# Attention's sums stored unturned, and normalised in the last phase

## The chip, the cores and the metric

One core of one Trainium2 chip. The metric is the device time of one execution in microseconds. Each figure is one number for the whole program: three phases that follow one another on five engines and overlap at their seams. The engines are TensorE (PE), VectorE (DVE), ScalarE (ACT), GpSimd (POOL) and SyncE (SP, which here issues all DMAs). Each runs its own list of instructions in order and waits on semaphores for the others.

## The reference

A block of three parts over x of shape (2, 2048, 256) in fp32:

```
x = x + 0.5 * ffn(layernorm(x))
x = x + attn(layernorm(x))
x = x + 0.5 * ffn(layernorm(x))
```

`ffn` is `square(relu(x W_fc^T)) W_proj^T` (1024 hidden channels), followed by five steps of a spiking neuron, whose count of spikes over 5 is the output. `attn` has 16 heads of 16 channels, rotary embedding on q and k, a causal softmax over 2048 keys, a bias on v and an output projection with bias:

```
scores = einsum('bhsd,bhtd->bhst', q, k) * scale      # causal mask
probs  = softmax(scores)
out    = einsum('bhst,bhtd->bhsd', probs, v)          # then x @ Wo.T + bo
```

## The kernel before, in words

**Phase A** (`feed_forward(True, ...)`) works in 8 chunks of CH = 512 tokens: the first ffn, the second layernorm, q, k and v. **Phase B** (`attention`) works in 8 groups: 2 batches times 4 groups of 4 heads. **Phase C** (`feed_forward(False, ...)`) does, for 8 chunks, the attention's output projection with its residual, then the second ffn.

*fp32 by halves.* A factor is split into a high part (`fp32r`, by ACT) and a low part (by DVE, value minus high); a product is three matmuls (hi x hi, lo x hi, hi x lo). `high` (L243 to 248) makes the high part, `low` (L359 to 362) the low part.

*Phase B.* A group has 4 steps j (512 queries each), a step has 4j + 4 blocks of 128 keys; a block is a slot, 40 slots a group, 320 in all (LAST). In each slot PE computes the block's scores for 4 heads (`scores`, L1078) into two buffers `s_ps`; ACT takes their exponentials into `probs` (L950); PE multiplies by the values (`products`, L1094) two slots later and sums in `o_ps`. The values carry a column of ones, so `o_ps` has, for each of 4 heads, 32 rows (VW): 16 channels, one row with the sum of the probabilities, 15 unused. Ahead of this, up to 20 slots earlier, PE computes all scores once more by 512 keys (`unit`, L1049) and DVE takes their maxima (L971, or L974 with the mask). These units go through three PSUM banks `m_ps` in a fixed order (`ring_order`, ORDER): the item number modulo 3 is the bank, PE waits for `max_read` of the item three before. From a step's maxima DVE makes shifts, which PE turns (`turn_shift`) and SP writes as rows of `qT`.

When a step's sums are complete, ACT copies `o_ps` to `osum` (`read_sum`, L938), with one buffer. Three slots into the next step an item "sums" stands in the ring: PE turns `osum` by four transposes of 128 x 128 (`turn_sums`, L1064), so that tokens are on the partitions, and DVE (`normalise`) takes the reciprocals of the sums (L1005, 16 numbers a partition) and multiplies (L1008) into `att`. SP stores this to `attn_tok` in DRAM (L816). The last two sums have their own bank (LATE); the very last is turned in phase C's first slot.

*Phase C.* A chunk is loaded from `attn_tok` (`load_attn`, L146) to `ain`, PE turns it back by eight transposes (`attn_turn`, `turn`, L572), ACT and DVE split it to `mT_hi` and `mT_lo`, PE projects (`attn_out`, L579), DVE adds the residual (`attn_sum`, L390), then stats, norm (`norm_scale` L340 to 348, `norm` L355), the transposes of `xn`, `xT_hi`/`xT_lo`, and the ffn. An iteration `it` has eight slots f (128 hidden channels each): PE does `up` f (six matmuls, L545) and `down` of three slots before (twelve, L563); ACT relu, square and `h_hi` (L294, L301, L303); DVE `h_lo` (L452); DVE also counts spikes of the chunk before (L373, one level a slot from f=3). `xT_hi` and `xT_lo` of the next chunk stand in f=7, and PE's `up` of f=0 waits for `xT_lo` (`pre_evac`). The attention's part runs ahead: in iteration `it`, f=1 has `attn_out(it+1)`, f=2 and f=4 the norm of chunk it+1, f=5 and f=6 the turn, `mT_hi` and `mT_lo` of chunk it+2.

The first two chunks' attention parts and the first norm are spread over the last group's 40 slots (`c_lead(x)`, x = slot - 280): each engine does its slot of phase B, then its piece of lead x. So x=19 is behind slot 299, the last that has maxima, and x=39 is behind the last slot.

Of the kernel before, what the change touches and what calls it, by code (L numbers as in the profile page):

```python
# [84 lines left out]
def feed_forward(first, src, dst, w, io, own, banks, s, meet):  # L85
# [15 lines left out]
    else:  # L101
        ain, xb, x2, bias = (own[n] for n in ("ain", "xb", "x2", "bias"))
# [22 lines left out]
    def sync(sp):  # L125
# [48 lines left out]
        def lead(x=None):  # L174
# [60 lines left out]
    def scalar(act):  # L235
# [5 lines left out]
        def high(which, c, hi, bank=tps):  # L241
# [24 lines left out]
        def lead(x=None):  # L266
# [8 lines left out]
            elif x == 21:  # L275
                high("a", 0, mT_hi, gps)
            elif x == 27:
                std(0)
            elif x == 29:
                high("a", 1, mT_hi, gps)  # L280
            elif x == 33:
                high("pre", 0, xT_hi, gps)

        def body(it, f):
# [21 lines left out]
            if not first and has(it, -2) and f == 5:  # L306
                high("a", it + 2, mT_hi, gps)
# [11 lines left out]
    def vector(dve):  # L319
# [39 lines left out]
        def low(which, c, hi, lo, bank=tps):  # L359
# [3 lines left out]
               .then_inc(s[which + "_evac"], 1)  # L363

# [48 lines left out]
        def lead(x=None):  # L413
# [12 lines left out]
            elif x == 22:  # L426
                low("a", 0, mT_hi, mT_lo, gps)
            elif x == 25:
# [3 lines left out]
            elif x == 28:  # L432
# [4 lines left out]
            elif x == 30:  # L437
                low("a", 1, mT_hi, mT_lo, gps)
            elif x == 34:
                low("pre", 0, xT_hi, xT_lo, gps)  # L440

        def body(it, f):
# [11 lines left out]
            if not first and f == 6 and has(it, -2):  # L454
                low("a", it + 2, mT_hi, mT_lo, gps)
# [27 lines left out]
            elif has(it, -1):  # L483
# [3 lines left out]
                if f == 4:  # L487
                    norm_scale(it + 1)
                    norm("pre", it + 1, it + 1, x2, xn, 0)

        return lead, body

    def gpsimd(pool):
# [22 lines left out]
        def lead(x):  # L516
# [3 lines left out]
            elif x == 27:  # L520
                add_bias(1)
# [14 lines left out]
    def tensor(pe):  # L536
# [12 lines left out]
        def down(it, f):  # L549

            if f == 0:
# [65 lines left out]
        def lead(x=None):  # L617
# [19 lines left out]
        def body(it, f):  # L637
# [26 lines left out]
            if not first and f == 5 and has(it, -2):  # L664
                attn_turn(it + 2)
# [15 lines left out]
MAX_FROM, MAX_TO, SUM = -20, 20, 3  # L681
# [60 lines left out]
LATE = [("sums", GROUPS - 1, j) for j in (NJ - 2, NJ - 1)]  # L742
assert [e for _, e in ORDER[-2:]] == LATE
# [5 lines left out]
def bank_of(e):  # L749
    return MB - 1 if e in LATE else ITEM[e] % MB  # L750
# [13 lines left out]
def attention(w, io, own, banks, s, ahead):  # L764
# [3 lines left out]
    probs, ident, bias, mask, masked, maxes, negmax, negparts, shiftT, osum, denom, att = (own[n] for n in (  # L768
        "probs", "ident", "bias_b", "mask", "masked", "maxes", "negmax", "negparts", "shiftT", "osum", "denom", "att"))
# [12 lines left out]
    def sync(sp):  # L782
# [177 lines left out]
    def vector(dve):  # L960
# [38 lines left out]
        def normalise(e):  # L999
            t, i = step_no(e[1], e[2]), ITEM[e]  # L1000
            dve.wait_ge(max_done, i + 1)
            if e in LATE:
# [375 lines left out]
```

## Time and profile before

| | |
|---|---|
| three runs, us | 1480.48, 1480.99, 1483.31 |
| the profiled execution, us | 1480.84 |
| its span, first to last instruction, us | 1479.1 |
| mean granted clock of TensorE | 0.949 |
| busy: PE, DVE, ACT, POOL | 91%, 77%, 58%, 15% |

Phase A ends at about 420 us, phase B at 1251.5 us, phase C at the span's end. Busy time is a share of the span; for PE it counts latencies too, so a PE that is busy all the time may still have small gaps. The granted clock is a share of 2.4 GHz: 0.50 is 1.2 GHz.

### The profile page before, as it was taken

The numbers are of one execution on the slowest core, as the hardware profiler recorded it, in microseconds if no ns is written. First come the engines' busy times: TensorE is split into PE (matmuls) and PEld (weight loads), VectorE is DVE, ScalarE is ACT, GpSimd is POOL, SyncE is SP. The second block draws the span as 40 slices with busy tenths as digits, with TensorE's granted clock in tenths as the row PEclk, the third lists the DMA queues.
The fourth block names the chain that finished last, engine by engine and source line by source line (L and its number), as shares of the span: only waits on it lengthen the run. The fifth ranks groups of instructions, "written<-read, shape, count | busy, mean of one in ns | idle before, by whom it ended". The sixth has DMA issues, their size and how long they took to land.

```text
span 1479.1 us, 22638 instructions
## 1 busy us (share of the span) xinstructions
PE 1345.1 (91%) x8416; PEld 809.8 (55%) x8416; DVE 1134.0 (77%) x2686; ACT 861.4 (58%) x1157; POOL 223.7 (15%) x205
## 2 busy tenths in 40 slices
PE   4988888967799999999999999999999998999996
PEld 3877777854444343444444444443443433999996
DVE  6566776796788888898898898888888851576675
ACT  4654455511166666676666666666666668665664
POOL 4002222241210110110110110110210110101100
PEclk9999999976699999999999999999999999999998
DMA  3123443772272160250340420610701011232312
GB/s 110 48 81 119 136 135 122 149 209 93 72 109 29 27 92 6 39 75 6 56 59 6 75 40 5 91 24 5 106 9 44 9 33 47 76 100 87 99 44 72
DMA packets 98598, 101.41 MB, mean 69 GB/s; under 512 B 39260, under 2 KB 78940, under 8 KB 96860
## 3 DMA queue, kind: packets, MB, share of 16 engines
q1 hardware_dynamic: 98488, 99.97, 29.7%
q8 instruction: 66, 1.08, 0.3%
q14 instruction: 44, 0.36, 0.1%
HBM read 60.16 MB, written 37.75 MB: 66 GB/s over the span
## 4 chain that ended last, share of the span: by engine, by line
PE 74%; DVE 19%; ACT 4%; issue 3%; DMA 0%; POOL 0%; SPq 0%; DVEq 0%; ACTq 0%
PE m_ps L1049 20%; PE o_ps L1094 18%; DVE maxes L971 9%; PE yps_c L563 6%; PE ups_c L545 6%; PE s_ps L1078 5%; PE ups_a L545 5%; PE yps_a L563 4%; PE gps_a L594 3%; DVE masked L974 3%; PE gps_a L579 2%; DVE turned_a L403 2%; PE gps_c L579 2%; ACT probs L950 1%; PE tps_a L572 1%
## 5 line engine op out<-in xcount | busy, mean ns | idle before, releaser
L950 ACT ACTIVATE probs<-s_ps 128x1024 f32<-128x1024 f32 (+3 forms) x640 | 542.0, 896 | 282.6 <-PE s_ps L1078 281.2
L971 DVE TENSOR_REDUCE maxes<-m_ps 128x1 f32<-128x512 f32 x768 | 490.2, 684 | 72.6 <-PE m_ps L1049 70.7
L1049 PE MATMUL m_ps<-kT,qT 64*128 64x512 f32 (+3 forms) x1280 | 455.6, 459 | 56.4 <-DVE maxes L971 37.9
L1049 PEld LDWEIGHTS m_ps<-kT,qT 64*128 64x128 f32 x1280 | 204.2, 192 | 412.1 <-DVE maxes L971 277.6
L1078 PE MATMUL s_ps<-qT,kT 64*128 64x512 f32 (+3 forms) x1280 | 317.0, 404 | 6.8 <-ACT probs L950 6.6
L1094 PE MATMUL o_ps<-probs,v_w 128*32 128x512 f32 (+3 forms) x2560 | 311.1, 559 | 0.1
L974 DVE CUSTOM_DVE_ANT_0 masked<-m_ps,mask 128x384 f32<-128x384 f32 (+3 forms) x512 | 233.6, 485 | 52.7 <-PE m_ps L1049 50.8
L919 POOL TENSOR_SCALAR_AFFINE_SELECT probs<-probs 128x512 f32<-128x512 f32 x128 | 81.3, 635 | 742.0 <-ACT probs L950 742.0
L1078 PEld LDWEIGHTS s_ps<-qT,kT 64*128 64x128 f32 x1280 | 170.0, 192 | 34.0 <-ACT probs L950 28.7
L452 DVE TENSOR_TENSOR h_lo_c<-hsq_c,h_hi_c 128x512 fp32r<-128x512 f32 x64 | 45.0, 703 | 71.1 <-ACT hsq_c L301 35.6
L294 ACT ACTIVATE relu_a<-ups_a 128x512 f32<-128x512 f32 x64 | 38.2, 596 | 99.5 <-PE ups_a L545 98.9
L452 DVE TENSOR_TENSOR h_lo_a<-hsq_a,h_hi_a 128x512 fp32r<-128x512 f32 x64 | 47.3, 739 | 58.5 <-ACT hsq_a L301 36.4
L1094 PEld LDWEIGHTS o_ps<-probs,v_w 128*32 128x32 f32 x2560 | 51.2, 109 | 73.6 <-issue 61.4
L294 ACT ACTIVATE relu_c<-ups_c 128x512 f32<-128x512 f32 x64 | 38.1, 596 | 73.5 <-PE ups_c L545 72.6
L501 POOL TENSOR_TENSOR rot_a<-turned_a 128x512 f32<-128x512 f32 x32 | 42.9, 1362 | 219.9 <-DVE turned_a L403 219.9
L563 PE MATMUL yps_a<-down_hi,h_hi_a 128*128 128x256 f32 x256 | 73.0, 285 | 2.2 <-ACT y_a L288 2.2
L563 PE MATMUL yps_c<-down_hi,h_hi_c 128*128 128x256 f32 x256 | 73.0, 285 | 0.0
L563 PE MATMUL yps_a<-down_lo,h_hi_a 128*128 128x256 f32 x256 | 72.5, 283 | 0.0
L563 PE MATMUL yps_a<-down_hi,h_lo_a 128*128 128x256 f32 x256 | 72.5, 283 | 0.0
L563 PE MATMUL yps_c<-down_hi,h_lo_c 128*128 128x256 f32 x256 | 72.4, 283 | 0.0
L563 PE MATMUL yps_c<-down_lo,h_hi_c 128*128 128x256 f32 x256 | 72.3, 283 | 0.0
L545 PE MATMUL ups_a<-xT_hi_a,up_hi 128*128 128x512 f32 x128 | 54.3, 424 | 2.5 <-DVE xT_lo_a L362 2.5
(128 smaller groups left out, 1923.3 us busy)
## 6 DMA issues: line engine op xcount, KB each, us to landing
qT<-qkT_parts SPq DMA_DIRECT2D x96, 128.0 KB
kT<-qkT_parts SPq DMA_DIRECT2D x48, 256.0 KB
qkT_parts<-qk_hi_a SPq DMA_DIRECT2D x32, 256.0 KB, 4.9
qkT_parts<-qk_lo_a SPq DMA_DIRECT2D x32, 256.0 KB, 4.6
table_a<-in_rot SPq DMA_DIRECT2D x8, 768.0 KB, 7.4
xin_a<-in_x SPq DMA_DIRECT2D x8, 512.0 KB, 3.9
xres_a<-in_x SPq DMA_DIRECT2D x8, 512.0 KB, 4.8
x<-xsum_a SPq DMA_DIRECT2D x8, 512.0 KB, 3.2
```

Source lines behind the costliest of these rows:

```text
L294: act.activation(relu[:, f % 2, :], ups[:, f % 2, :], ACT.Relu).then_inc(s["relu_done"], 1)
L452: dve.tensor_tensor(h_lo[:, f % HB, :], hsq[:, f % 2, :], h_hi[:, f % HB, :].bitcast(F32), ALU.subtract).then_inc(s["lo_done"], 1)
L545: last = pe.matmul(ups[:, f % 2, :], wt[:, c, f * P:(f + 1) * P], x[:, c, :], start=(i == 0), stop=(i == 3 * EC - 1))
L563: last = pe.matmul(yps[:, t, :], h[:, f % HB, t * P:(t + 1) * P], wt[:, f, :], start=(f == 0 and i == 0 and t % 2 == 0), stop=(f == FC - 1 ...
L579: last = pe.matmul(out, x[:, c, t * P:(t + 1) * P], wt[:, c, c0:c1], start=(i == 0), stop=(i == 3 * EC - 1))
L919: pool.affine_select(out=tile, in_=tile, compare_op=ALU.is_ge, fill=0.0, base=0, pattern=[[0, G], [1, P]], channel_multiplier=-1).then_inc ...
L950: act.activation(probs[:, b % PBUF, 2 * hp:2 * hp + 2, off:CH], s_ps[hp][:, :, off:CH], ACT.Exp, scale=D ** -0.5).then_inc(exp_done, 1)
L971: dve.tensor_reduce(out, m_ps[:, i % MB, 0:width], AX.X, ALU.max).then_inc(max_read, 1)
L974: dve.tensor_tensor_reduce(masked[:, i % MB, 0:width], m_ps[:, i % MB, 0:width], mask[:, CH - width:CH], 1.0, NEG, ALU.add, ALU.max, out). ...
L1049: pe.matmul(m_ps[:, i % MB, 0:width], qT[n % 2][r0:r0 + HR, j, hp, t * P:(t + 1) * P], kT[n % 2][r0:r0 + HR, hp, k * CH:k * CH + width], s ...
L1078: mm = pe.matmul(s_ps[hp][:, par, off:CH], kT[n % 2][r0:r0 + HR, hp, b * P:(b + 1) * P], qT[n % 2][r0:r0 + HR, j, hp, off:CH], start=True, ...
L1094: mm = pe.matmul(o_ps[VW * h:VW * (h + 1), off:CH], v_w[n % 2][:, b, h, :], probs[:, b % PBUF, h, off:CH], start=(b == 0), stop=(b == T * ...
```

## The change

- Phase B: the items "sums" leave the ring, and with them `turn_sums`, `normalise`, `att`, `denom`, LATE and the last sums in phase C's first slot. `osum` has two buffers, `read_sum` waits for the store of two steps before, and SP stores `osum` as it is, 128 rows (channels and the row of sums), to `sumsT` in DRAM.
- Phase C: `load_attn` makes four transfers a chunk: for each half k of the channels, the 8 heads' 16 rows to `sums`, and the row of the sums of each head, repeated for its 16 channels, to `denom`. DVE inverts `denom` and multiplies (`attn_norm`), ACT and DVE split `sums` (`attn_high`, `attn_low`). The transposes of `ain` go.
- The pieces of the lead move: `load_attn(0)` from x=0 to x=2; `attn_norm(0)` at x=19; `attn_high(0)` 20, `attn_low(0)` 21, `attn_out(0)` 22 (was 23), `attn_sum(0)` 24 (25), `attn_norm(1)` 25, `norm` 27 (28), `attn_high(1)` 28 (29), `attn_low(1)` 29 (30), the turn of `xn` 29 (31), `xT_hi` 30 (33), `xT_lo` 31 (34).
- `count` and `denom` change places in memory.

```diff
@@ feed_forward, sync
         def load_attn(c):
-            wait(sp, "a_T", c)
+            wait(sp, "a_evac", c)
             j, n = c % (NC // B), (c // (NC // B) + 1) * NG
-            sp.wait_ge(meet["att_out"][j % 2], 16 * (NC // B // 2 * (n - 1) + j // 2 + 1))
-            sp.dma_start(ain[:, :, :], rows(io["attn"], c)).then_inc(s["a_in"], 16)
+            sp.wait_ge(meet["osum_out"][j % 2], 16 * (NC // B // 2 * (n - 1) + j // 2 + 1))
+            if c == 0:
+                sp.wait_ge(meet["pv_done"], meet["blocks_but_last"])
+            heads = io["sumsT"][:, :, c * CH:(c + 1) * CH].rearrange("(k g) (h r) t -> k (g h) r t", k=EC, h=G)
+            for k in range(EC):
+                sp.dma_start(sums[:, k, :], heads[k, :, 0:D, :]).then_inc(s["a_in"], 16)
+                sp.dma_start(denom[:, k, :], heads[k, :, D:D + 1, :].broadcast_to([H // EC, D, CH])).then_inc(s["a_in"], 16)
@@ scalar
+        def attn_high(c):
+            wait(act, "a_norm", c + 1)
+            wait(act, "o_done", c)
+            act.activation(mT_hi[:, :, :], sums[:, :, :], ACT.Copy).then_inc(s["a_hi"], 1)
...
             if not first and has(it, -2) and f == 5:
-                high("a", it + 2, mT_hi, gps)
+                attn_high(it + 2)
@@ vector
+        def attn_norm(c):
+            wait(dve, "a_in", 16 * 2 * EC * (c + 1))
+            dve.reciprocal(denom[:, :, :], denom[:, :, :]).then_inc(s["a_rec"], 1)
+            wait(dve, "a_rec", c + 1)
+            dve.tensor_tensor(sums[:, :, :], sums[:, :, :], denom[:, :, :], ALU.mult).then_inc(s["a_norm"], 1)
+
+        def attn_low(c):
+            wait(dve, "a_hi", c + 1)
+            dve.tensor_tensor(mT_lo[:, :, :], sums[:, :, :], mT_hi[:, :, :].bitcast(F32), ALU.subtract).then_inc(s["a_evac"], 1)
...
                 if f == 4:
                     norm_scale(it + 1)
                     norm("pre", it + 1, it + 1, x2, xn, 0)
+                    if has(it, -2):
+                        attn_norm(it + 2)
@@ tensor
-        def attn_turn(c):
-            wait(pe, "a_in", 16 * (c + 1))
-            wait(pe, "x2_done", c)
-            turn(ain, "a_T", gps)
-
         def attn_out(c):
             wait(pe, "a_evac", c + 1)
+            wait(pe, "x2_done", c)
@@ attention
         def store(n, j):
             tok, group = place(n)
-            sp.wait_ge(max_read, ITEM["sums", n, j] + 1)
-            sp.dma_start(io["attn"][tok + j * CH:tok + (j + 1) * CH, group * G * D:(group + 1) * G * D]
-                         .rearrange("(t p) n -> p t n", p=P), att[:, j % 2, :, :]).then_inc(att_out[j % 2], 16)
+            sp.wait_ge(o_read, step_no(n, j) + 1)
+            sp.dma_start(io["sumsT"][group, :, tok + j * CH:tok + (j + 1) * CH], osum[:, j % 2, :]).then_inc(osum_out[j % 2], 16)
@@ attention, scalar
+            t = step_no(n, j)
             act.wait_ge(pv_done, block_no(n, j, T * j + T))
-            if (n, j) != (0, 0):
-                act.wait_ge(max_done, ITEM["sums", (NJ * n + j - 1) // NJ, (j - 1) % NJ] + 1)
-            act.activation(osum[:, :], o_ps[:, :], ACT.Copy).then_inc(o_read, 1)
+            wait(act, osum_out[j % 2], 16 * (t // 2))
+            act.activation(osum[:, j % 2, :], o_ps[:, :], ACT.Copy).then_inc(o_read, 1)
```

## Rows read from the trace of the kernel before

**Rows 1.** The page's chain of waits, shares of the span by engine and line.

```profile
PE 74%; DVE 19%; ACT 4%; issue 3%; DMA 0%; POOL 0%; SPq 0%; DVEq 0%; ACTq 0%
PE m_ps L1049 20%; PE o_ps L1094 18%; DVE maxes L971 9%; PE yps_c L563 6%; PE ups_c L545 6%; PE s_ps L1078 5%; PE ups_a L545 5%; PE yps_a L563 4%; PE gps_a L594 3%; DVE masked L974 3%; PE gps_a L579 2%; DVE turned_a L403 2%; PE gps_c L579 2%; ACT probs L950 1%; PE tps_a L572 1%
```

**Rows 2.** Windows: us, busy of PE, PEld, DVE, ACT, POOL, clock, DMA share, GB/s.

```profile
500.00:600.00 100.00, 95.55 (x631) 41.16 (x627) 87.53 (x235) 64.94 (x80) 14.83 (x18) 0.97 0.30 44
...
1200.00:1250.00 50.00, 44.19 (x289) 17.12 (x293) 10.70 (x27) 38.62 (x46) 8.92 (x9) 0.90 0.19 56
...
1350.00:1400.00 50.00, 49.99 (x337) 45.39 (x336) 35.04 (x63) 30.52 (x51) 5.67 (x2) 1.00 0.33 106
```

**Rows 3.** Groups by form: shapes, count, busy us, mean ns, idle before.

```profile
L1064 PE MATMUL m_ps<-ident,osum 128*128 128x128 f32 x128 | 20.9, 286 | 0.0
...
L1005 DVE RECIPROCAL denom<-m_ps 128x16 f32<-128x16 f32 x32 | 8.0, 251 | 7.1 <-PE m_ps L1064 6.9
```

**Rows 4.** Timeline of one step's sums: start, us, engine, line.

```profile
425.76 0.42 PEld L1064 LDWEIGHTS m_ps<-ident,osum 128*128 128x128 f32 x4 [0.25 <-issue]
425.77 0.66 PE L1064 MATMUL m_ps<-ident,osum 128*128 128x128 f32 x4
...
427.08 0.25 DVE L1005 RECIPROCAL denom<-m_ps 128x16 f32<-128x16 f32 x1
...
427.70 1.88 DVE L971 TENSOR_REDUCE maxes<-m_ps 128x1 f32<-128x512 f32 x3
```

**Rows 5.** Groups by form on DVE: small operations and one of 1024.

```profile
L381 DVE SCALAR_TENSOR_TENSOR xsum_c<-count_c,xres_c 128x1024 f32<-128x1024 bf16 x8 | 9.8, 1221 | 0.1
...
L340 DVE RECIPROCAL ln_c<-ln_c 128x4 f32<-128x4 f32 x8 | 1.4, 172 | 1.0 <-ACT ln_c L239 1.0
...
L340 DVE RECIPROCAL ln_a<-ln_a 128x8 f32<-128x8 f32 x5 | 1.0, 191 | 0.0
...
L342 DVE TENSOR_TENSOR ln_a<-ln_a 128x8 f32<-128x8 f32 x5 | 0.8, 168 | 0.2
```

**Rows 6.** Timeline of DVE in one iteration of phase C.

```profile
1348.36 0.69 DVE L452 TENSOR_TENSOR h_lo_c<-hsq_c,h_hi_c 128x512 fp32r<-128x512 f32 x1 [1.75 <-ACT hsq_c L301]
...
1352.40 0.69 DVE L452 TENSOR_TENSOR h_lo_c<-hsq_c,h_hi_c 128x512 fp32r<-128x512 f32 x1
...
1355.49 1.22 DVE L362 TENSOR_TENSOR mT_lo_c<-gps_c,mT_hi_c 128x1024 fp32r<-128x1024 f32 x1
...
1358.26 1.22 DVE L362 TENSOR_TENSOR xT_lo_c<-tps_c,xT_hi_c 128x1024 fp32r<-128x1024 f32 x1 [0.42 <-ACT xT_hi_c L248]
```

**Rows 7.** Timeline of PE: two starts of `up` f=0, and `ain`'s turn.

```profile
1331.87 0.50 PE L545 MATMUL ups_c<-xT_hi_c,up_hi 128*128 128x512 f32 x1
...
1350.55 1.03 PE L572 MATMUL gps_c<-ident,ain_c 128*128 128x128 f32 x8
...
1359.53 0.50 PE L545 MATMUL ups_c<-xT_hi_c,up_hi 128*128 128x512 f32 x1
```

**Rows 8.** Timeline of ACT in the same iteration.

```profile
1351.62 1.03 ACT L248 ACTIVATE mT_hi_c<-gps_c 128x1024 fp32r<-128x1024 f32 x1 [0.52 <-PE gps_c L572]
...
1361.23 0.60 ACT L294 ACTIVATE relu_c<-ups_c 128x512 f32<-128x512 f32 x1 [1.97 <-PE ups_c L545]
...
1362.40 0.62 ACT L303 ACTIVATE h_hi_c<-relu_c 128x512 fp32r<-128x512 f32 x1
```

**Rows 9.** Timelines of ACT, DVE and PE in slots 299 to 304.

```profile
1203.63 1.51 ACT L950 ACTIVATE probs<-s_ps 128x768 f32<-128x768 f32 x2 [0.69 <-PE s_ps L1078]
...
1200.71 0.67 DVE L409 TENSOR_TENSOR proj_lo_c<-stage_o_c,proj_hi_c 128x512 fp32r<-128x512 f32 x1
...
1211.19 0.73 PE L1078 MATMUL s_ps<-qT,kT 64*128 64x512 f32 x4
```

**Rows 10.** PE behind an idle stretch (timeline), and the clock there (windows).

```profile
1226.08 1.71 PE L1078 MATMUL s_ps<-qT,kT 64*128 64x512 f32 x4 [2.36 <-ACT probs L950]
...
1226.00:1232.00 6.00, 5.80 (x24) 1.47 (x24) 1.41 (x2) 5.32 (x7) 0.00 (x0) 0.50 0.56 179
```

**Rows 11.** DMA issues: size, median us to landing.

```profile
ain_c<-attn_tok SPq DMA_DIRECT2D x8, 512.0 KB, 3.9
```

More of the change, by code:

```diff
@@ L101, in feed_forward @@
     else:
-        ain, xb, x2, bias = (own[n] for n in ("ain", "xb", "x2", "bias"))
+        sums, denom, xb, x2, bias = (own[n] for n in ("sums", "denom", "xb", "x2", "bias"))
         split = [("o", own["stage_o"][:, :], proj_hi, proj_lo)]
@@ L425, in lead @@
                 split_low(0)
-            elif x == 22:
-                low("a", 0, mT_hi, mT_lo, gps)
-            elif x == 25:
+                attn_norm(0)
+            elif x == 21:
+                attn_low(0)
+            elif x == 24:
                 attn_sum(0)
@@ L431, in lead @@
                 norm_var(0)
-            elif x == 28:
+            elif x == 25:
+                attn_norm(1)
+            elif x == 27:
                 norm_scale(0)
@@ L436, in lead @@
                 norm("pre", 0, 0, x2, xn, 0)
-            elif x == 30:
-                low("a", 1, mT_hi, mT_lo, gps)
-            elif x == 34:
+            elif x == 29:
+                attn_low(1)
+            elif x == 31:
                 low("pre", 0, xT_hi, xT_lo, gps)
@@ L663, in body @@
                 up(it, 0)
-            if not first and f == 5 and has(it, -2):
-                attn_turn(it + 2)
         return lead, body
@@ L767, in attention @@
     qT, kT, v_in, v_w = ([own[f"{n}{p}"] for p in range(2)] for n in ("qT", "kT", "v_in", "v_w"))
-    probs, ident, bias, mask, masked, maxes, negmax, negparts, shiftT, osum, denom, att = (own[n] for n in (
-        "probs", "ident", "bias_b", "mask", "masked", "maxes", "negmax", "negparts", "shiftT", "osum", "denom", "att"))
+    probs, ident, bias, mask, masked, maxes, negmax, negparts, shiftT, osum = (own[n] for n in (
+        "probs", "ident", "bias_b", "mask", "masked", "maxes", "negmax", "negparts", "shiftT", "osum"))
     s_ps, m_ps, o_ps = banks
@@ L822, in moves @@
                     shift(n, j)
-                elif what == "sums":
+            for n, j in steps():
+                if g == min(block_no(n, j, T * j + T) + STORE, LAST):
                     store(n, j)
@@ L997, in shift_out @@
             dve.tensor_copy(shiftT[:, :], m_ps[0:2 * G * T, i % MB, 0:P]).then_inc(max_read, 1)
[L999 to L1002, printed above, removed]
-                dve.wait_ge(max_read, i)
-            sums = m_ps[:, bank_of(e), :].rearrange("p (g w) -> p g w", w=VW)
-            dve.reciprocal(denom[:, :].unsqueeze(2), sums[:, :, D:D + 1]).then_inc(denom_done, 1)
-            dve.wait_ge(denom_done, t + 1)
-            wait(dve, att_out[t % 2], 16 * (t // 2))
-            dve.tensor_tensor(att[:, e[2] % 2, :, :].rearrange("p t (h d) -> p (t h) d", d=D), sums[:, :, 0:D],
-                              denom[:, :].unsqueeze(2).broadcast_to([P, T * G, D]), ALU.mult)\
-               .then_inc(max_read, 1)
         pending = []
@@ L1032, in free_bank @@
         def free_bank(e):
[L1033 removed]
+            wait(pe, max_read, ITEM[e] - MB + 1)
         def unit(e):
@@ L1126, in end @@
                 products(*SLOTS[g])
-        def last_sums():
-            ring(ITEMS[LAST])
-        return slot, end, last_sums
+        return slot, end
     return sync, scalar, vector, gpsimd, tensor
@@ L1178, in build @@
     for n, shape in (("masked", [P, MB, CH]), ("maxes", [P, 2, 2, G // 2, T, NJ]), ("negmax", [P, G * T]), ("negparts", [P, 2, G * T]),
-                     ("shiftT", [2 * G * T, P]), ("denom", [P, T * G]), ("att", [P, 2, T, G * D])):
+                     ("shiftT", [2 * G * T, P])):
         b[n] = memory.take(n, shape)
@@ L1184, in build @@
     b["probs"] = memory.take("probs", [P, PBUF, G, CH])
-    b["osum"] = memory.take("osum", [P, CH])
+    b["osum"] = memory.take("osum", [P, 2, CH])
     assert memory.at <= rest
@@ L1192, in build @@
     for n, shape, dt in (("stage_o", [P, EC * E], F32), ("proj_hi", [P, EC, E], F32R), ("proj_lo", [P, EC, E], F32R), ("bias", [P, E], F32),
-                         ("ain", [P, T, E], F32), ("xin", [P, T, E], F32), ("mT_hi", [P, EC, CH], F32R), ("mT_lo", [P, EC, CH], F32R),
+                         ("sums", [P, EC, CH], F32), ("xin", [P, T, E], F32), ("mT_hi", [P, EC, CH], F32R), ("mT_lo", [P, EC, CH], F32R),
                          ("xb", [P, T, E], F32), ("x2", [P, T, E], F32), ("stats", [P, T, 6], F32), ("mv", [P, T, 2], F32),
@@ L1200, in build @@
                          ("hsq", [P, 2, CH], F32), ("h_hi", [P, HB, CH], F32R), ("h_lo", [P, HB, CH], F32R), ("y", [P, T * E], F32),
-                         ("count", [P, T * E], BF16)):
+                         ("denom", [P, EC, CH], F32)):
         c[n] = memory.take(n + "_c", shape, dt)
@@ L1204, in build @@
     memory = Memory(nc, probs)
-    for n in ("xres", "xsum"):
-        c[n] = memory.take(n + "_c", [P, T, E])
+    for n, shape, dt in (("xres", [P, T, E], F32), ("xsum", [P, T, E], F32), ("count", [P, T * E], BF16)):
+        c[n] = memory.take(n + "_c", shape, dt)
     with ExitStack() as ctx:
```

87 lines of the change are left out of this document (28 added, 59 removed).

## The prediction

> **What bounds the kernel now.** I read the chain of waits first, for the lines that set the end [rows 1]: TensorE (PE) has 74%, VectorE (DVE) 19%, ScalarE (ACT) 4%, DMA nothing. DVE's share is `maxes` (L971, L974), the attention's maxima. Then the busy times by stretch, since shares over the span mix stages [rows 2]. Between 500 and 600 us PE is busy 95.6 and DVE 87.5 of 100: they hand three PSUM banks to and fro, and both matter. In the last 20 slots (1200 to 1250) no maxima are left, DVE is busy 10.7 of 50 and ACT 38.6. In the last phase (1350 to 1400) PE is busy 49.99 of 50 and DVE 35.0. So three stages, and the change touches all.
>
> **1. Attention: the turned sums go.** 32 steps lose four transposes on PE (128 in all), and a reciprocal (0.25 us each) and a product on DVE [rows 3]. In one step [rows 4] the four transposes take 0.66 us with the last one's latency; at 0.14 us for one weight load to the next (their row in [rows 4] has 0.42 for the four, which overlap) it is 0.55 us of PE at the most. DVE starts the reciprocal at 427.08 and the next maximum at 427.70: 0.62 us, and never idles between. Both partners of the ring lose nearly the same, so whichever is late there gains about 0.6 us. 30 of the 32 steps lie among maxima (the last two come in slot 307 and behind the last slot, where DVE is idle): 30 x 0.6 = **-18 us**. Bounds: 12 us if part is lost to other waits of PE on bank 2 and 3, 22 us if PE's wait on `att` goes too. The store now goes out of `osum`, which has two buffers and is next written two steps, twelve slots at the least, later; it writes 128 rows of 2 KB where 512 pieces of 256 B were written, and ACT's copy no longer waits for PE. Nothing of that is waited for: 0.
>
> **2. The reciprocal of 128x1024.** It is new: DVE must now invert and multiply [128, 2, 512] for each of eight chunks. Three shapes of a reciprocal stand in the trace: 4 elements 172 ns, 8 elements 191 ns [rows 5], 16 elements 251 ns [rows 3]; a product of 8 costs 168 ns [rows 5]. So an element of a reciprocal costs far more than the 1.04 ns that 1221 ns for 1024 elements (about 157 ns fixed) make of an ordinary operation. Slopes: 4.75 ns from 4 to 8, 7.5 from 8 to 16, 6.6 over all. For 1024: 5.0 us by the first; 6.6 x 1020 + 172 = 6.9 us over all; 7.8 us by the second; and if the slope rises once more by as much, to 10.3 ns, 10.6 us. The 16-element row reads PSUM, so part of its excess may be the source; I take the middle, **R = 6.9 us**, bounds 5.0 and 10.6. The product is 1.2 us, as the two-input row of 1024 [rows 5].
> By the Trainium skill, "VectorE: DVE Perf Modes", section "First, the fixed hardware budget", a reciprocal is an iterative divide with a repeat count of 8. If that means 8 cycles of the page's 0.96 GHz for each element, the estimate is 8.5 us and the fixed part, and the sum below would end at 1545 us; the rows have shown 4.75 to 7.5 ns an element, not yet its 8.3.
>
> **3. The last phase, iterations 0 to 5.** PE loses eight transposes of `ain` (1.03 us with the last one's latency, 0.8 to the next start) [rows 7]. DVE gains R + 1.2 behind the normalisation of slot f=4. By sums this would fit: DVE's 35.0 of 50 [rows 2] is 19.4 of the 27.66 us between two starts of `up` f=0 (1331.87, 1359.53) [rows 7]; 19.4 + 8.1 = 27.5. But the order forbids it. ACT's `attn_high` of f=5 waits for the product (`a_norm`); queued behind it on ACT are relu, squares and `h_hi` of f=6, relu of f=7 and `xT_hi`; on DVE, behind the product, `h_lo` of f=5, `h_lo` of f=6 (which needs ACT's), `mT_lo`, a spike, `xT_lo`; PE's `up` f=0 waits for `xT_lo`. Before, this chain ended at 1358.26 + 1.22 = 1359.48 and PE started at 1359.53: it has no slack. After, from PE's start (1331.87): 16.49 to `h_lo` f=4 (1348.36), 4.04 until DVE has normalised (1352.40) [rows 6]; R + 1.2; `attn_high` 1.03 and relu to `h_hi` 1361.23 to 1363.02 = 1.79 [rows 8]; `h_lo` 0.65, `mT_lo` and a spike 2.35 (1355.49 to 1357.84, where the idle 0.42 before `xT_lo` begins), `xT_lo` 1.22 [rows 6], about 0.15 of semaphores. That is 28.9 + R = 35.8 us against 27.66: +8.1, six times **+48.6 us** (37 at R = 5.0, 71 at R = 10.6). With h_hi and h_lo in four buffers, PE can go on to `down` f=4 and then waits.
>
> **4. The clock.** In this chain PE waits about 5 us for `up` f=0: from the product's end it is 7.2 us (1.03 + 1.79 + 0.65 + 2.35 + 1.22 + 0.15), and PE has only `down` f=5 left, which follows `h_lo` f=5 (0.65) and takes about 1.5. In the last 20 slots PE idled 2.36 us and was then granted 0.50 (1.2 GHz) for the six us from 1226 to 1232 [rows 10]; six us at half rate lose 3.0 of PE's work. Here PE sets the time between `up` f=0 and f=4, so it would be paid: I take 2.5 us a time, six times **+15 us** (0 if the level holds, 20 at most).
>
> **5. The last slots (lead).** `attn_norm(0)` stands at x=19, behind `split_low` (1200.71 + 0.67 = 1201.4); with R + 1.2 it ends at 1209.5, `attn_high(0)` at x=20 at 1210.6. Queued behind it on ACT are the exponentials of slot 301, which before began at 1203.63: +7.0 [rows 9]. PE's two score buffers are then full, `attn_out(0)` at x=22 follows slot 302, and slot 304's scores, before at 1211.19, come at about 1217.8: +6.6. The second `ain` turn and the turn of slot 307 are gone, 0.8 and 0.55 us of PE: -1.4. The new hole of some 7 us before `attn_out` can cost the clock there, +1. `attn_norm(1)` (x=25) starts near 1220, 3.8 us after `attn_out(0)` has ended, and would end near 1229, before ACT's x=28 (near 1231): hidden, but by 2 us only; at R = 10.6 some of it shows. Sum **+6** (bounds 0 and +12). The removed last turn is 0.55 us of PE, within that.
> **Loads.** SP issues four transfers of 256 KB a chunk for one of 512 KB: +0.5 MB, at the start of an iteration; in front of `load_x`. SP passes them as soon as `mT_lo` of the chunk before is done (f=6), some 20 us before their use at f=4; a load of `ain` landed after 3.9 us in the median [rows 11]: 0. `load_attn(0)` moves from x=0 to x=2 and waits for the end of group 6, 17 slots ahead of use: 0. `load_attn(1)` is issued near 1211.5 and needed near 1220, the only close one.
>
> **Sum**, against the profiled execution (1480.84, span 1479.1 and 1.7 around it): 1480.84 - 18 + 48.6 + 15 + 6 = 1532.4; the median of the runs shown, 1480.99, lies 0.15 above that execution. **Forecast 1532 us.**
>
> **Rivals.**
> - *The slope goes on rising* as it did from 4.75 to 7.5 ns; halfway from 7.5 to 10.3, at 8.9 ns, R = 9.2. Against it: the 16-element row reads PSUM. 6 x (28.9 + 9.2 - 27.66) = 63, clock 15, lead 8, attention -18: 1549 us. The Trainium skill's repeat count (same page and section) would end between this and the forecast.
> - *Cheap reciprocal*: what looks like a slope is fixed cost, and 1024 elements take 1.2 us as other operations do. Then the chain is 28.9 + 1.2 = 30.1, +2.4 x 6 = 15, lead nothing, the clock held: 1480.8 - 18 + 15 = 1478 us, barely on the other side. It decides at R near 1.8, without clock loss: 6 x (R + 1.24) = 18. Against it: 19 ns for four elements more, and another 60 for eight more.
> - *DVE's idle time takes it all*: if ACT and DVE were far enough ahead, the iteration would be DVE's 27.5 us, as now, and the lead 0: 1480.8 - 18 - 1 = 1462 us, faster. For it: DVE idles 30% of the phase. Against it: `xT_lo` ends 0.05 us before PE's `up` now.
> - *The loads come late*: the broadcast rows of `denom` take over 20 us to land, and DVE waits 3 to 6 us more in each of six iterations: 1550 to 1568. For it: a shape that the trace doesn't show; against it: the 3.9 us of `ain` [rows 11].
>
> **Chances.** Forecast 0.55, rising slope 0.30, loads late 0.06, cheap reciprocal 0.05, all hidden 0.04. Range: R = 5.0 with half of the clock's loss gives 1480.8 - 20 + 37 + 7 + 3 = 1508, and with none of it 1500; R = 10.6 gives 1480.8 - 15 + 71 + 15 + 10 = 1562. So 1500 to 1560, of which about 2 in 10 are left out, most of it below. A measurement of this kernel tells about 0.2%, 3 us. Slower 0.90, the same 0.02 (between the cheap reciprocal with and without its clock loss), faster 0.08.
>
> **What would show it.** The row of the new reciprocal, 128x1024, eight times: 6.9 us each. In 1300 to 1350 PE's busy share falls from all to under 85%, and a stretch at 0.50 appears. Two starts of `up` f=0 are 35 to 38 us apart for six iterations, then 27.7. ACT waits for DVE `sums` at `attn_high`, PE's weight load waits for DVE `xT_lo` some 5 us at a time. The attention's stretch up to the last maximum is about 18 us shorter. A row below 2 us for the reciprocal makes the forecast wrong; a period of 27 us beside a long reciprocal makes part 3 wrong.

## The result: slower by 2.4%, 1518.9 us

The changed kernel took 1518.91 us (median of 4 runs, 1515.61 to 1519.26) against 1482.15 (1480.48 to 1483.62); ratio 1.0243, 95% interval [1.0224, 1.0263]. Forecast was 1532, range 1500 to 1560. The profiled execution has a span of 1516.9 us, 37.8 more than before.

Its page begins with the busy times. Then the chain of waits, whose rows answer to [rows 1]:

```profile
PE 1328.0 (88%) x8224; PEld 798.4 (53%) x8224; DVE 1174.4 (77%) x2638; ACT 860.2 (57%) x1157; POOL 223.2 (15%) x205
...
PE 66%; DVE 24%; ACT 6%; issue 4%; DMA 0%; DVEq 0%; POOL 0%; SPq 0%; ACTq 0%
PE m_ps L1040 19%; PE o_ps L1077 17%; DVE maxes L977 9%; PE ups_a L572 5%; PE ups_c L572 5%; PE s_ps L1061 5%; PE yps_a L589 4%; DVE masked L980 3%; PE yps_c L589 3%; PE gps_a L620 3%; DVE denom_c L378 3%; PE gps_a L605 2%; DVE turned_a L425 2%; PE gps_c L605 2%; PE tps_a L598 1%
```

PE has less to do (17 us less busy, 192 matmuls less) and the kernel is slower: PE's share of the chain fell from 74% to 66%, and a new member stands in it, `denom_c` L378, the reciprocal, with 3%. DVE's share of busy time, 77%, has not moved at all; it would have told nothing. The windows that answer to [rows 2]:

```profile
500.00:600.00 100.00, 95.13 (x641) 39.97 (x640) 88.48 (x239) 68.29 (x83) 14.82 (x18) 1.00 0.30 50
...
1200.00:1250.00 50.00, 45.63 (x295) 25.03 (x288) 17.52 (x38) 38.42 (x52) 5.38 (x5) 0.93 0.16 48
...
1300.00:1350.00 50.00, 41.91 (x243) 37.04 (x243) 31.85 (x43) 21.61 (x37) 5.67 (x2) 0.85 0.40 124
1350.00:1400.00 50.00, 42.06 (x257) 37.27 (x257) 36.52 (x61) 23.49 (x40) 2.84 (x1) 0.90 0.21 64
```

In the last phase PE is busy 42 of 50 us instead of 50, at a mean clock of 0.85 to 0.90 instead of 1.00: it waits, and the waits cost the clock. Who is waited for stands in the list of that phase's waits (the last three figures are us in total, times, and the longest in us):

```profile
ACT mT_hi_c L258 <- DVE sums_c L380: 54.9, 6, 9.2
...
PEld ups_c L572 <- DVE xT_lo_c L372: 25.9, 7, 4.9
...
PEld yps_c L589 <- DVE h_lo_c L477: 23.7, 6, 4.4
```

To part the 37.8 us by stage, two events mark the seams: the last maximum's `negmax` (DVE, step j = 3 of each group) and PE's first `up` of the last phase. From the timeline of DVE, before (the last two of eight), then after:

```profile
1093.31 0.22 DVE L981 TENSOR_REDUCE negmax<-maxes 128x16 f32<-128x64 f32 x1
1199.41 0.22 DVE L981 TENSOR_REDUCE negmax<-maxes 128x16 f32<-128x64 f32 x1
```

```profile
558.99 0.22 DVE L987 TENSOR_REDUCE negmax<-maxes 128x16 f32<-128x64 f32 x1
660.23 0.22 DVE L987 TENSOR_REDUCE negmax<-maxes 128x16 f32<-128x64 f32 x1
763.76 0.22 DVE L987 TENSOR_REDUCE negmax<-maxes 128x16 f32<-128x64 f32 x1
...
1173.29 0.22 DVE L987 TENSOR_REDUCE negmax<-maxes 128x16 f32<-128x64 f32 x1
```

and of PE, before and after:

```profile
1251.53 0.50 PE L545 MATMUL ups_c<-xT_hi_c,up_hi 128*128 128x512 f32 x1
```

```profile
1231.09 0.50 PE L572 MATMUL ups_c<-xT_hi_c,up_hi 128*128 128x512 f32 x1
```

| stage | before | after | difference | forecast |
|---|---|---|---|---|
| to the last maximum | 1199.4 | 1173.3 | -26.1 | -18 |
| from there to the first `up` (lead) | 52.1 | 57.8 | +5.7 | +6 |
| last phase | 227.6 | 285.8 | +58.2 | +63.6 |
| span | 1479.1 | 1516.9 | +37.8 | +51.6 |

**The reciprocal.** The group of the new instruction, by form (count, busy us and mean ns, idle time before it):

```profile
L378 DVE RECIPROCAL denom_c<-denom_c 128x1024 f32<-128x1024 f32 x8 | 52.3, 6543 | 0.0
```

It takes 6.54 us, eight times, and DVE is never idle ahead of it: the loads were in time.

**One iteration.** The same places on DVE and ACT as in [rows 6, 8], with the two starts of `up` f=0 at its ends, as in [rows 7]. DVE, where the first row is `h_lo` of f=4 and the last `xT_lo`:

```profile
1318.60 0.69 DVE L477 TENSOR_TENSOR h_lo_c<-hsq_c,h_hi_c 128x512 fp32r<-128x512 f32 x1 [1.75 <-ACT hsq_c L311]
...
1322.65 6.55 DVE L378 RECIPROCAL denom_c<-denom_c 128x1024 f32<-128x1024 f32 x1
1329.23 1.23 DVE L380 TENSOR_TENSOR sums_c<-sums_c,denom_c 128x1024 f32<-128x1024 f32 x1
1330.37 0.68 DVE L477 TENSOR_TENSOR h_lo_c<-hsq_c,h_hi_c 128x512 fp32r<-128x512 f32 x1
...
1336.18 1.22 DVE L372 TENSOR_TENSOR xT_lo_c<-tps_c,xT_hi_c 128x1024 fp32r<-128x1024 f32 x1
```

ACT, and then PE's weight loads:

```profile
1330.49 1.06 ACT L258 ACTIVATE mT_hi_c<-sums_c 128x1024 fp32r<-128x1024 f32 x1 [9.15 <-DVE sums_c L380]
```

```profile
1299.62 0.29 PEld L572 LDWEIGHTS ups_c<-xT_hi_c,up_hi 128*128 128x128 f32 x1 [4.85 <-DVE xT_lo_c L372]
1337.45 0.29 PEld L572 LDWEIGHTS ups_c<-xT_hi_c,up_hi 128*128 128x128 f32 x1 [4.71 <-DVE xT_lo_c L372]
```

ACT stands still for 9.15 us until the product is there, PE for 4.7 us until `xT_lo` is. The distance is 37.83 us, against 27.66 in [rows 7]. From PE's start to `h_lo` of f=4 it takes 18.98 us (1299.62 to 1318.60), where the prediction had 16.49: the 2.49 us more are what the low clock costs (e3_keep_busy, below). From there to the reciprocal it is 4.05 us, as worked out.

### The profile page after: what moved, and what is told of

It is laid out like the page before. It is cut to its first block, busy times and chain, and to the rows that moved or that the text cites. A ratio compares the mean times of both kernels' runs of the same rounds, so it can differ in the third digit from the quotient of the medians.

```text
span 1516.9 us, 22165 instructions
## 1 busy us (share of the span) xinstructions
PE 1328.0 (88%) x8224; PEld 798.4 (53%) x8224; DVE 1174.4 (77%) x2638; ACT 860.2 (57%) x1157; POOL 223.2 (15%) x205
## 4 chain that ended last, share of the span: by engine, by line
PE 66%; DVE 24%; ACT 6%; issue 4%; DMA 0%; DVEq 0%; POOL 0%; SPq 0%; ACTq 0%
PE m_ps L1040 19%; PE o_ps L1077 17%; DVE maxes L977 9%; PE ups_a L572 5%; PE ups_c L572 5%; PE s_ps L1061 5%; PE yps_a L589 4%; DVE masked L980 3%; PE yps_c L589 3%; PE gps_a L620 3%; DVE denom_c L378 3%; PE gps_a L605 2%; DVE turned_a L425 2%; PE gps_c L605 2%; PE tps_a L598 1%
## 5 line engine op out<-in xcount | busy, mean ns | idle before, releaser
L1040 PE MATMUL m_ps<-kT,qT 64*128 64x512 f32 (+3 forms) x1280 | 443.5, 454 | 57.6 <-DVE maxes L977 39.6
L1040 PEld LDWEIGHTS m_ps<-kT,qT 64*128 64x128 f32 x1280 | 198.8, 190 | 408.7 <-DVE maxes L977 279.2
L1061 PE MATMUL s_ps<-qT,kT 64*128 64x512 f32 (+3 forms) x1280 | 312.7, 399 | 12.8 <-ACT probs L956 12.5
L572 PE MATMUL ups_c<-xT_hi_c,up_hi 128*128 128x512 f32 x128 | 57.4, 449 | 24.0 <-DVE xT_lo_c L372 24.0
```

What stands on the lines that cost most here:

```text
L572: last = pe.matmul(ups[:, f % 2, :], wt[:, c, f * P:(f + 1) * P], x[:, c, :], start=(i == 0), stop=(i == 3 * EC - 1))
L1040: pe.matmul(m_ps[:, i % MB, 0:width], qT[n % 2][r0:r0 + HR, j, hp, t * P:(t + 1) * P], kT[n % 2][r0:r0 + HR, hp, k * CH:k * CH + width], s ...
L1061: mm = pe.matmul(s_ps[hp][:, par, off:CH], kT[n % 2][r0:r0 + HR, hp, b * P:(b + 1) * P], qT[n % 2][r0:r0 + HR, j, hp, off:CH], start=True, ...
```

## The experiments

In all, "distance" is the time between two PE starts of `up` f=0 of the last phase; `e1` to `e3` are edits of the changed kernel.

### The length of the reciprocal (e1_narrow)

```diff
-dve.reciprocal(denom[:, :, :], denom[:, :, :])
+dve.reciprocal(denom[:, :, 0:32], denom[:, :, 0:32])
```

> The changed kernel (1518.9 us, last phase 285.8 us from PE's first `up`) with the reciprocal cut to 64 of its 1024 elements; the other sums stay undivided, so part of the normalisation is left out. Everything else, the product at f=4 too, stays in its place. Theory (the long reciprocal stands in the chain up f=0, norm at f=4, product, mT_hi on ACT, relu and h_hi f=6, xT_lo, next up f=0, which is 28.9 + R us): R falls from 6.54 to 0.5 to 0.6, the chain to 29.5, so the distance of two up f=0 falls from 37.7 to 29.5 us if the clock holds, 31.7 if PE's remaining wait of some 3 us still costs it; the lead gives back about 6 us. Together 1518.9 - 6 x 6 to 8.2 - 6 = 1464 to 1477 us. Rival 1 (the reciprocal's length is hidden and four loads a chunk or the extra traffic cost the time): no change, 1515 to 1519. Rival 2 (DVE's idle time takes what is left, order does not matter): distance 27.7 or less, 1458 or less.

Measured 1474.65 us (ratio to before 0.9954, [0.9939, 0.9969]). The reciprocal's row, and two of the five equal distances:

```profile
L378 DVE RECIPROCAL denom_c<-denom_c 128x64 f32<-128x64 f32 x8 | 4.3, 543 | 2.2 <-DMA denom_c<-sumsT 2.2
```

```profile
1283.68 0.19 PEld L572 LDWEIGHTS ups_c<-xT_hi_c,up_hi 128*128 128x128 f32 x1 [2.77 <-DVE xT_lo_c L372]
1314.60 0.19 PEld L572 LDWEIGHTS ups_c<-xT_hi_c,up_hi 128*128 128x128 f32 x1 [2.77 <-DVE xT_lo_c L372]
```

The distance is 30.9 us, and the iteration behind the sixth takes 28.24 against 26.78 before: 1.45 us of clock. 30.93 - 1.45 = 29.48, the chain's 28.9 + 0.54 = 29.44. So 44 us of the kernel hang on six microseconds of an instruction. The loads and the traffic are those of the changed kernel, so rival 1 falls; the one wait for a load, the 2.2 us in the row above, lies ahead of the last phase (at 1193 us). And it is not all: with the short reciprocal the distance is still 3.3 us over the 27.66 of before, 1.45 of it clock and the rest the chain, since the product at f=4 still stands ahead of ACT's `mT_hi`. Rival 2 (DVE's idle time takes what is left) falls too.

### The place (e2_early)

```diff
@@ vector, body
             if not first and f == 6 and has(it, -2):
                 attn_low(it + 2)
+            if not first and f == 1 and has(it, -2):
+                attn_norm(it + 2)
...
-                    if has(it, -2):
-                        attn_norm(it + 2)
```

> The changed kernel with nothing left out, only the normalisation (reciprocal and product, 7.8 us) of iterations 0 to 5 moved on DVE from behind the norm of f=4 to behind h_lo of f=1. Theory (order): ACT's mT_hi at f=5 no longer waits for it; what is then late is DVE itself, whose work in an iteration is 19.4 + 7.8 = 27.2 us and is nearly all strung together from f=1 on, so a distance of 28 to 30.5 us instead of 37.7: 1518.9 - 6 x 7.2 to 9.7 = 1461 to 1476 us. Rival (it is the amount, DVE 7.8 us more in a phase it has no room for, wherever it stands): 34 us or more, above 1497.

Measured 1484.32 us (1.0007, [0.9991, 1.0023]): no change against before, 35 us under the changed kernel, but 8 above my expectation. The distances are 28.9, 31.65, 30.16, 31.28, 30.17, 31.31, at or a little over the upper end of the expected 30.5, and far from the rival's 34. The three over 31 each hold one stretch at 0.50 (near 1291, 1353 and 1414 us), the two of 30.2 hold none, so that 1.1 to 1.5 us of the three go with the clock. Two weight loads of `up` f=0:

```profile
1296.88 0.19 PEld L572 LDWEIGHTS ups_c<-xT_hi_c,up_hi 128*128 128x128 f32 x1 [0.20 <-DVE xT_lo_c L372]
1327.04 0.19 PEld L572 LDWEIGHTS ups_c<-xT_hi_c,up_hi 128*128 128x128 f32 x1 [0.59 <-DVE xT_lo_c L372]
```

and, among the waits from 1240 to 1450 us:

```profile
ACT ln_c L246 <- DVE ln_c L343: 30.8, 6, 6.2
...
PEld tps_c L598 <- DVE xn_c L365: 14.3, 6, 2.9
```

Now ACT waits for DVE's part of the norm, and PE for the normalised `xn`, not for the attention's halves: here the long instruction delays what stands behind it at f=1 too, and f=1 is only the better place. Seven of the ten us between a distance of 37.7 and before's 27.7 went by the place alone, with the same work. The kernel's other excess lies ahead of the last phase: its last maximum came at 1178.6 us instead of 1173.3, with the same code up to there (see part 1 below).

### The clock (e3_keep_busy)

```diff
+        def keep_busy(c):
+            wait(pe, "x2_done", c)
+            for i in range(17):
+                pe.matmul(gps[:, 0, :], up_hi[:, 0, 0:P], up_hi[:, 0, 0:CH], start=True, stop=True)
...
+            if not first and f == 7 and has(it, -2):
+                keep_busy(it + 2)
             if f == 0 and has(it, 0):
+                if not first and 1 <= it <= NC - 2:
+                    keep_busy(it + 1)
                 up(it, 0)
```

> The changed kernel, nothing left out, with 17 extra matmuls of 512 columns (3.9 us at the full clock) on PE in each of its two waits of an iteration: behind down f=4, where it waits 4.2 us for h_lo, and ahead of up f=0, where it waits 4.6 us for xT_lo. Their results are overwritten and never read. Theory (2.25 us of each distance are the low clock behind these waits): the granted clock stays at 1.00 through the last phase, the distances fall from 37.7 to 35.4 us, the iteration behind the sixth from 29.0 to 26.8: -13.5, 1505 us. Rival (the 2.25 us are something else, such as a longer way from xT_lo to PE or late relus): distances 37.7 or more, 1519 to 1525.

Measured 1506.1 us (1.0167, [1.0147, 1.0186]): 34 matmuls an iteration whose results nobody reads make the kernel 13 us faster. In the profiled execution the last phase alone is 13.1 us shorter (272.7 instead of 285.8); its whole span is only 8.4 us shorter, as what lies ahead of that phase took 4.7 us longer. In the changed kernel the window from 1332 to 1342, with the second wait and what follows it, had a clock of 0.52; with them the last phase is at 1.00:

```profile
1332.00:1342.00 10.00, 5.58 (x18) 4.32 (x17) 6.02 (x7) 5.16 (x10) 0.00 (x0) 0.52 0.38 114
```

```profile
1300.00:1440.00 140.00, 136.94 (x836) 120.49 (x835) 105.95 (x147) 65.21 (x112) 9.69 (x4) 1.00 0.30 91
```

```profile
1338.22 0.19 PEld L572 LDWEIGHTS ups_c<-xT_hi_c,up_hi 128*128 128x128 f32 x1 [1.19 <-DVE xT_lo_c L372]
1373.57 0.19 PEld L572 LDWEIGHTS ups_c<-xT_hi_c,up_hi 128*128 128x128 f32 x1 [1.19 <-DVE xT_lo_c L372]
```

The distance is 35.35; the chain of the prediction with the measured R is 28.9 + 6.54 = 35.44. The iteration behind the sixth takes 26.79, as before the change. So 2.25 to 2.5 us of each distance from the third to the sixth, and as much behind it, were the low level. Where they are paid shows in PE's rows, from the start of `up` f=0 to the first matmul behind its twelve, in the changed kernel and with the matmuls added:

```profile
1337.45 0.79 PE L572 MATMUL ups_c<-xT_hi_c,up_hi 128*128 128x512 f32 x1 [4.42 <-DVE xT_lo_c L372]
1342.69 0.29 PE L605 MATMUL gps_c<-proj_hi_c,mT_hi_c 128*128 128x256 f32 x1
```

```profile
1338.22 0.50 PE L572 MATMUL ups_c<-xT_hi_c,up_hi 128*128 128x512 f32 x1 [0.77 <-DVE xT_lo_c L372]
1341.08 0.28 PE L605 MATMUL gps_c<-proj_hi_c,mT_hi_c 128*128 128x256 f32 x1
```

The twelve take 5.24 us instead of 2.86: 2.38 us. The low level itself lasted some 10 us, but PE waited for nearly half of them, and that half cost nothing more. It fell near 1332.4, behind the first wait (for `h_lo`) and before the second (for `xT_lo`); this run fills both, so which of them brings the fall is not parted.

### Which partner of the ring gains (e6_turn_one, e7_no_product)

Both are edits of the kernel before.

```diff
@@ e6_turn_one, turn_sums
-            for t in range(T):
+            for t in range(1):
@@ e7_no_product, normalise
+            if t > 1:
+                dve.sem_inc(max_read, 1)
+                return
```

> The kernel before (distance of two groups' last maxima 106.05 us, each with one stretch at the low clock) with one of the four transposes of osum in each sum's item; the other three columns blocks are left out of the result. It takes 0.42 us of PE a step and nothing of DVE, and the item keeps its place and bank. Theory (at a sum's item both partners of the ring are late, and each one's saving shows only as far as the other's): 0.2 to 0.4 us a step, 0.8 to 1.7 a group, 104.4 to 105.3 us, -6 to -13 us in all. Rival 1 (DVE alone sets the attention's pace): distance 106.0, no change. Rival 2 (PE alone): 104.4 or less.

> The kernel before with DVE's product of 256 elements left out in all but the first two steps (att keeps old values); the four transposes, the reciprocal of 16 and the item stay. It takes 0.37 us of DVE a step and nothing of PE. Theory (as for the run with one transpose): 0.2 to 0.37 us a step, 0.8 to 1.5 a group, 104.5 to 105.3 us. Rival 1 (DVE alone): 104.5, the whole 0.37 a step. Rival 2 (PE alone): 106.0. Together with that run: if either saving alone gives nothing, only both together give the 2.54 us a group of the change.

With one transpose the kernel took 1481.69 us (0.9994, [0.9984, 1.0003]), without the product 1471.41 (0.9928, [0.9902, 0.9955]). The `negmax` rows of two neighbouring groups in each:

```profile
881.31 0.22 DVE L981 TENSOR_REDUCE negmax<-maxes 128x16 f32<-128x64 f32 x1
987.25 0.22 DVE L981 TENSOR_REDUCE negmax<-maxes 128x16 f32<-128x64 f32 x1
```

```profile
458.15 0.22 DVE L981 TENSOR_REDUCE negmax<-maxes 128x16 f32<-128x64 f32 x1
563.36 0.22 DVE L981 TENSOR_REDUCE negmax<-maxes 128x16 f32<-128x64 f32 x1
```

Three transposes of four gone from PE: 105.9 us a group instead of 106.05, 0.04 us a step of the 0.42 saved. The product gone from DVE: 105.2 in the groups with the same clock as before, 0.21 us a step of 0.37. So my theory that either saving shows in part was wrong for PE, whose transposes were nearly free while the item stood, and right for DVE at its lower end; that DVE alone sets the pace would have given 0.37. The whole item gone gives 0.63 a step (part 1 below), as much as DVE's 0.62 of [rows 4], but 0.04 and 0.21 do not add up to it: no run parts the rest, which holds the reciprocal of 16, the last transpose and the item's turn in the ring.

### A version that beats both (e5_compact), and two attempts on it

The sums of a chunk, 16 heads by 512 tokens, are 128 x 64 numbers when each is there once; the change inverts each of them 16 times. Here SP loads them as 128 x 64, DVE inverts that one iteration earlier, SP stores 16 rows, and `denom` is loaded repeated from those; the product stands at f=1.

```diff
+        def load_comp(c):
+            ...
+            heads = io["sumsT"][:, :, c * CH:(c + 1) * CH].rearrange("g (h r) (q t) -> (g h) r q t", h=G, q=8)
+            sp.dma_start(comp[:, c % 2, :], heads[:, D, :, :]).then_inc(s[f"c_in{c % 2}"], 16)
+        def attn_rec(c):
+            ...
+            dve.reciprocal(crec[:, c % 2, :], comp[:, c % 2, :]).then_inc(s["a_rec"], 1)
+        def store_rec(c):
+            ...
+            sp.dma_start(io["recT"][:, c * CH:(c + 1) * CH].rearrange("h (q t) -> h q t", q=8), crec[:, c % 2, :])\
+              .then_inc(s[f"r_out{c % 2}"], 16)
```

> A version meant to be better, nothing left out: the sums of the probabilities of a chunk are loaded as 128 x 64 (each once, not 16 times), inverted by one reciprocal of 64 elements an iteration earlier, stored to DRAM as 16 rows, and loaded repeated from there; the product of 1024 stands behind h_lo of f=1. Theory: the last phase is bound by PE again, without the turns of ain, 26.6 us an iteration against 27.66 before the change; attention keeps its 26 us; the lead loses nothing: 1482.2 - 26 - 6 = 1450 us. Rival 1 (attention's 26 us come in part from the clock and don't recur with other phases): up to 1457. Rival 2 (the round through DRAM, two DMAs and SP's waits, is late): DVE waits for the loads at f=1 and the distance is 29 us or more, above 1465.

Measured 1451.04 us (0.9787, [0.9771, 0.9803]). It is 31 us faster than before and 68 faster than the changed kernel.

```profile
L409 DVE RECIPROCAL crec_c<-comp_c 128x64 f32<-128x64 f32 x8 | 4.3, 542 | 0.0
```

```profile
1254.00:1416.00 162.00, 160.65 (x1056) 145.21 (x1055) 126.33 (x216) 99.18 (x167) 12.00 (x5) 1.00 0.37 105
```

PE is busy 160.65 of 162 us at the full clock, distances 26.8 to 27.4. The 0.2 to 0.8 us over 26.6 are not fully explained. DVE waits 8.0 us in all for the repeated rows ahead of the product, but only 3.1 of them in the last phase (1.42, 1.35 and 0.29 us, in the distances 27.4, 27.3 and 27.0); a distance of 27.1 has no such wait.

> The compact version (1451.0 us, distances 27.4, 27.3, 27.0, 27.1, 26.8 in the last phase) with the product of 1024 behind h_lo of f=3 instead of f=1. At f=1 DVE waited 8 us in all for the repeated rows to land, and the product took 1499 ns in the mean instead of 1225, beside GpSimd's add. Theory (both slow it and push xT_lo of f=7 past PE): at f=3 the loads have landed and GpSimd is done, the distances fall to 26.8, -1 to -2 us in all, 1449 to 1450. Rival (DVE's work between f=3 and f=7 is what is late, so that a product there is worse than at f=1): distances 28 or more, 1455 or more.

The edit is `f == 3` for `f == 1`. Measured 1454.18 us (0.9808, [0.9794, 0.9823]), no better: the product took 1214 ns instead of a mean of 1499 (one of 3.43 us, beside GpSimd's add, and seven of 1.2), DVE no longer waited for the rows in this phase, and the distances are 27.9, 27.4, 27.7, 26.8, 26.8, 26.8: three longer, three as good. The theory of a gain falls, and the rival's figure was not reached either.

> The compact version with the score matmuls of the first two slots of each group done three times over (the same values again, 16 matmuls more a group, about 1.5 us of PE): the place where PE waits for maxima of 128 columns and, 1 to 3 us later, the granted clock falls to 0.50 for 4 to 8 us in six of seven groups. Theory (these waits bring the fall, and a fall costs 2.3 us of a group): the stretches go, groups take 101.2 us and the added matmuls' share not hidden, 0.5 to 1 us: 6 x 2.3 - 8 x 0.75 = -8, 1443 us. Rival (the fall comes from the whole stretch of narrow matmuls before it, and these few change nothing): stretches stay, and the matmuls cost up to 12 us, 1455 to 1463.

```diff
-                mm = pe.matmul(s_ps[hp][:, par, off:CH], ...)
+                for _ in range(3 if j == 0 and b < 2 else 1):
+                    mm = pe.matmul(s_ps[hp][:, par, off:CH], ...)
```

Measured 1460.78 us (0.9853, [0.9838, 0.9869]): slower than e5_compact. The clock fell in every group all the same, and groups took 102.9 to 105.0 us. The expectation also counted wrong: in e5_compact only four of the seven distances (table below) hold such stretches, not six, and all seven are 11 us over seven undisturbed ones. The time is the rival's: the matmuls before decide, or the place is the wrong one; what brings the fall in the attention stays open.

## Why the prediction was right, and where its sizes were off

**The direction and the mechanism** (parts 2 and 3) held, with one thing left open (the first distance, below). R was read as 6.9 us from three short reciprocals; it is 6.54. The longer ones give the law: (6543 - 543) / 960 = 6.25 ns an element over 0.14 us, which makes 0.17 and 0.19 us for 4 and 8 as in [rows 5], and 0.24 for 16, where [rows 3] has 0.25. The overall slope of 6.6 was thus nearly right, and the rival "the slope goes on rising" falls: a few ns above and below the law at 4, 8 and 16 elements had looked like a rise. Whether the 8 ns at 16 come from its source in PSUM no run shows. What also falls is the reading of the Trainium skill's repeat count of 8 ("VectorE: DVE Perf Modes", "First, the fixed hardware budget") as 8 cycles an element, an estimate of 8.3 ns: the measured rows decide, 6.25 ns. The chain 28.9 + R was confirmed in three kernels, at two values of R: 35.35 (R = 6.54, e3), 29.48 (R = 0.54, e1, less the clock), and 37.7 less 2.25 in the changed kernel. That DVE's sum would fit in its idle time was rightly set aside.

**Part 4, the clock:** 2.5 us a time was forecast; 2.24 was paid by the iteration behind the sixth, where nothing else differs (29.02 against 26.78), and e3 took back 13 us of the 15. The six us at half rate of [rows 10] were near the right size for the work that PE does at the low level (5.24 us here), though the level itself lasts longer, over the wait too.

**Part 3, the number of times:** the last phase was forecast 5.4 us too slow. 0.36 us of R, six times, is 2.2. The clock is paid six times, but one distance late, from the second to the one behind the sixth, and came to 13.2 us (e3) instead of 15: 1.8. The rest, 1.2 us, is in the first distance, which grew by 6.6 us, where the chain with the measured R had 7.8; why is not shown.

**Part 5, the lead:** +6 forecast, +5.7 measured. `attn_norm(0)` held ACT for 6.20 us (its `mT_hi` began at 1183.02, 9.7 behind the last maximum) where 7.0 were worked out. The smaller terms of this part were not measured one by one.

**Part 1, the attention, is the mis-sized term:** -18 us (12 to 22) forecast, -26.1 measured. The saving itself was right: a group took 106.05 us, each with one stretch of some 7 us at the low clock (seven of seven), and takes 103.50 where such a stretch is left: 2.55 us, 0.63 a step, 17.8 in seven groups. But in three of the seven groups the stretch is gone, and these take 101.24: 2.27 us less each, 6.8 together (the rest, 1.5 us, lies in the first group and in the shorter stretch of the second). I had taken the clock of the attention as given. The kernel before has one stretch in each of the seven, and so has e6_turn_one, whose item still stands. Six kernels with the changed attention have between one and three groups with none, and most of them one with two, not in the same groups from kernel to kernel. So fewer stretches seem to come with the change, for a reason that no run shows. The part of luck in this one execution shows in the sums: the seven distances make 717.0 us in the changed kernel and to 719.4 to 721.4 in the five others, against 742.3 before. Of the 26.1 us some 2 to 4 are thus luck.

| kernel | distances of neighbouring groups, us |
|---|---|
| before | 106.1 106.0 106.0 106.0 106.1 106.1 106.1 |
| after | 102.7 101.2 103.5 101.3 103.5 101.2 103.5 |
| e1_narrow | 102.6 101.2 103.5 102.6 101.2 103.5 106.0 |
| e2_early | 102.7 101.2 103.5 102.6 105.1 102.6 102.7 |
| e3_keep_busy | 102.7 106.0 101.2 103.5 101.2 103.5 101.3 |
| e5_compact | 102.7 101.2 103.5 106.0 101.2 103.4 102.0 |
| e8_product_f3 | 102.6 101.2 103.5 102.6 105.9 101.2 104.3 |

101.2 goes with no stretch, 102.6 with one about half as long, 103.5 with one of some 7 us, 105 to 106 with two. The last groups of e5_compact (102.0, none) and e8_product_f3 (104.3, one) lie 0.8 us above; they alone also hold the first small reciprocals. Between after and e2_early these distances make 3.4 us of the 5.3 by which the last maximum comes later; 1.8 us lie ahead of the first of them. What sets the stretches is not shown; it is a matching of windows of the granted clock with distances, no experiment.

## What to carry to other kernels

Before moving an operation to another engine's idle time, write down the chain that runs through its place, on all engines, with the present slack; idle time in sums (here 30% of DVE) says nothing when every engine works its list in order. Take out repetition before the expensive operation, not after it: 64 reciprocals a partition and two small DMAs replaced 1024. And a wait of a few microseconds on TensorE cost more here than itself: with two waits of some four us in an iteration, TensorE also did five us of work at half rate and lost 2.4. A rough estimate should carry both. (The 68 us between the changed kernel and e5_compact are the shorter reciprocal and the product's earlier place together.)

## What was not expected of the hardware

- A reciprocal of fp32 takes 6.25 ns an element on DVE (543 ns for 64, 6543 for 1024, both from and to SBUF), against 1225 ns for a product of 1024.
- Matmuls added in PE's waits, whose results nobody reads, made the kernel 13 us faster.
- DVE beside GpSimd: the low half of `sums`, all in SBUF, takes 1.22 us, but 3.14 once, when it began while GpSimd's add ran. From e5_compact's timelines of DVE and POOL:

```profile
1182.97 3.14 DVE L414 TENSOR_TENSOR mT_lo_c<-sums_c,mT_hi_c 128x1024 fp32r<-128x1024 f32 x1 [0.93 <-ACT mT_hi_c L283]
1250.28 1.22 DVE L414 TENSOR_TENSOR mT_lo_c<-sums_c,mT_hi_c 128x1024 fp32r<-128x1024 f32 x1
```

```profile
1182.67 2.37 POOL L575 TENSOR_TENSOR xb_c<-xin_c,bias_c 128x1024 f32<-128x1024 f32 x1
```

The add ended at 1185.04 and DVE's instruction at 1186.11, 1.07 us later, a little less than one undisturbed duration. The product of 1024 did the same once: it began at 1237.05, 0.49 us into an add, and took 3.43 us instead of 1.23. In both it looks as if DVE stood still until the add had ended; no run tests it. Before, DVE read these values out of PSUM, and the eight took 1219 ns in the mean.
